# Five of eight layer-norm transposes moved from TensorE to the DMA queue

## The reference

```
h = layernorm(x)
Q, K, V = h Wq^T, ctx Wk^T, ctx Wv^T
x = x + tanh(g_xattn) * (softmax(causal(Q K^T / sqrt(128))) V) Wd^T
x = x + tanh(g_ffn) * (layernorm(x) W^T + bias)      W: 512x512, unpacked from 6-bit fields
```

## Time and profile before

| | |
|---|---|
| median of three runs | 1070.28 us (1069.42 to 1071.28) |
| the profiled execution's own time | 1069.89 us |
| its span in the profile | 1067.7 us, so 2.19 us lie around it |
| busy: PE, DVE, ACT, POOL | 1026.9, 677.1, 476.4, 235.3 us |

### The profile page before, as it was taken

The page is one execution under the profiler, slowest core; times in us unless marked ns, Lnnn a source line. Parts: engine busy times, 40 slices in busy tenths (PEclk is TensorE's granted clock), DMA queues, the critical chain, the costliest instruction groups (busy, mean ns, idle before and its releaser), DMA issues.

```text
span 1067.7 us, 20167 instructions
## 1 busy us (share of the span) xinstructions
PE 1026.9 (96%) x8002; PEld 577.5 (54%) x8002; DVE 677.1 (63%) x1364; ACT 476.4 (45%) x937; POOL 235.3 (22%) x245
## 2 busy tenths in 40 slices
PE   5889999999999999999999999999999999999995
PEld 2455555555555555555555555555555555555552
DVE  5856677776668556655566566555556664555578
ACT  5777676676434243343334323254433423333322
POOL 1355566566503100010003110010000400000003
PEclk9999999999999999999999999999999999999999
DMA  7747645445245133233321443312323332233211
GB/s 273 234 154 266 216 169 169 159 158 167 91 139 197 51 129 118 107 112 118 119 86 54 178 159 118 119 42 98 119 99 119 119 117 67 75 119 117 81 41 59
DMA packets 64250, 137.08 MB, mean 128 GB/s; under 512 B 5408, under 2 KB 38176, under 8 KB 53536
## 3 DMA queue, kind: packets, MB, share of 16 engines
q1 hardware_dynamic: 64160, 135.81, 37.2%
HBM read 93.85 MB, written 25.17 MB: 111 GB/s over the span
## 4 chain that ended last, share of the span: by engine, by line
PE 87%; DVE 7%; ACT 3%; issue 2%; DMA 1%; SPq 0%; POOL 0%; DVEq 0%; ACTq 0%; POOLq 0%
PE pa L1225 42%; PE py L1225 29%; PE av L1338 5%; PE pp L1321 3%; PE ps L1305 2%; PE py L1399 2%; PE pp L1305 2%; PE av L1375 1%; DVE q L843 1%; DMA raw_q<-in_wqT 1%; DVE sc L900 1%; DVE row_max L887 1%; DVE sc L889 1%; DVE sc L883 1%; DVE xh L1006 1%
## 5 line engine op out<-in xcount | busy, mean ns | idle before, releaser
L1225 PE MATMUL pa<-xT,wq 128*128 128x512 f16 x1536 | 342.7, 379 | 7.3 <-DVE q L843 4.5
L1225 PE MATMUL py<-wd,att 128*128 128x512 f16 x1488 | 337.0, 379 | 0.8 <-issue 0.8
L1225 PEld LDWEIGHTS pa<-xT,wq 128*128 128x128 f16 x1536 | 145.8, 98 | 187.6 <-issue 20.4
L1225 PEld LDWEIGHTS py<-wd,att 128*128 128x128 f16 x1488 | 142.9, 98 | 158.1 <-issue 1.1
L629 ACT ACTIVATE q<-pa 128x512 f16<-128x512 f32 x128 | 75.7, 592 | 246.6 <-PE pa L1225 246.6
L922 DVE SCALAR_TENSOR_TENSOR xacc<-py,f_y,xacc 128x512 f32<-128x512 f32 x128 | 95.8, 749 | 134.0 <-PE py L1225 134.0
L675 ACT ACTIVATE att<-av 128x256 f16<-128x256 f32 x256 | 80.8, 384 | 145.7 <-PE av L1338 145.3
L913 DVE SCALAR_TENSOR_TENSOR att<-av,att 128x256 f16<-128x256 f32 x256 | 93.5, 418 | 67.1 <-ACT att L675 66.9
L843 DVE SCALAR_TENSOR_TENSOR q<-pa,q 128x512 f16<-128x512 f32 x128 | 87.8, 686 | 63.6 <-ACT q L629 60.8
L1225 PE MATMUL pa<-wv,cT 128*128 128x128 f16 x1536 | 96.2, 219 | 0.0
L1225 PEld LDWEIGHTS pa<-wv,cT 128*128 128x128 f16 x1536 | 89.8, 98 | 0.9
(11 more groups left out here) (127 smaller groups left out, 1100.2 us busy)
## 6 DMA issues: line engine op xcount, KB each, us to landing
wq<-kept_q SPq DMA_DIRECT2D x24, 1024.0 KB, 7.2
wd<-kept_d SPq DMA_DIRECT2D x23, 1024.0 KB, 4.8
v_dup<-v_nat SPq DMA_DIRECT2D x128, 128.0 KB, 2.4
raw_d<-in_wdT SPq DMA_DIRECT2D x8, 1024.0 KB, 10.5
kept_q<-wq SPq DMA_DIRECT2D x8, 1024.0 KB, 7.5
kept_d<-wd SPq DMA_DIRECT2D x8, 1024.0 KB, 5.4
raw_q<-in_wqT SPq DMA_DIRECT2D x7, 1024.0 KB, 5.2
wk<-kept_k SPq DMA_DIRECT2D x24, 256.0 KB, 7.4
```

What stands on the lines that cost most here:

```text
L1225: last = pe.matmul(out, stationary(a, i), moving(b, i), start=(i == 0 and (a, b) == PASSES[0]), stop=(i == count - 1 and (a, b) == PASSES[ ...
```

## The change

Calls 2 to 6 of the norms are no longer transposed by PE (`BY_PE` keeps calls 0, 1 and 7). SP issues DMA transposes instead, from `xh` straight into `xT`: 8 a tile, two tiles in each of the two steps after the norm's own step, 16 in a step and 32 for a call, queued behind the reloads of that step's weights and ahead of `duplicate_v`. PE's 160 transposes of these calls and ACT's 20 copies out of `av` go. Whoever reads `xT` waits for the DMA semaphore `xT_ld` instead of `xT_ok`, and so does ACT before it overwrites `xh` in the next call. The FFNs of blocks 0 and 1 move from step 1 to step 3 of the pass, and their stores with them. The interleaving of the norms of kind 2 moves from the read of the transpose to the writes of `ln_hi` and `ln_lo` (views of innermost length 4, whose elements lie 128 apart).

```diff
+        FINAL = len(NORMS) - 1
+        BY_PE = (0, 1, FINAL)
...
+        def transposed(eng, call):
+
+            if call in BY_PE:
+                eng.wait_ge(xT_ok, tile_count(TILES * (call + 1) - 1) + 1)
+            else:
+                eng.wait_ge(xT_ld, 16 * 2 * KC * TILES * (call - 1))
...
+        def dma_tiles(n):
+
+            g, tb = n % GROUPS, n // GROUPS
+            if tb > 0 and g in (1, 2):
+                return NORMS.index((2, tb - 1)), (2 * g - 2, 2 * g - 1)
+            if 0 < tb < BLOCKS - 1 and g in (5, 6):
+                return NORMS.index((1, tb + 1)), (2 * g - 10, 2 * g - 9)
+            return None
...
-            if g == 1 and 0 < tb < BLOCKS - 1:
+            if g == 3 and 0 < tb < BLOCKS - 1:
                 return tb - 1
...
+            def transpose_tiles(call, tiles):
+
+                which, tb = NORMS[call]
+                if which == 1:
+                    sp.wait_ge(q_mm, 4 * GROUPS * (tb - 1))
+                    sp.wait_ge(f_mm, TILES * (tb - 1))
+                else:
+                    sp.wait_ge(q_mm, 4 * GROUPS * (tb + 1))
+                for t in tiles:
+                    sp.wait_ge(x_hi, TILES * call + t + 1)
+                    wait_x_lo(sp, TILES * call + t)
+                    for c in (HI, LO):
+                        for i in range(KC):
+                            sp.dma_start(xT[:, tb % 2, c, i, t * P:(t + 1) * P], xh[:, t, c, i * P:(i + 1) * P],
+                                         transpose=True).then_inc(xT_ld, 16)
...
                 if GROUPS <= m + 1 < STEPS:
                     back_qkv(m + 1)
+                if dma_tiles(n) is not None:
+                    transpose_tiles(*dma_tiles(n))
                 if m < STEPS:
                     duplicate_v(m)
...
+                return part.rearrange("p (j i) -> p i j", j=KC)
...
-                pool.tensor_tensor(xh[:, t % TILES, LO, :], xn[:, t % TILES, :], xh[:, t % TILES, HI, :],
-                                   ALU.subtract).then_inc(x_lo, 1)
+                pool.tensor_tensor(permuted(xh[:, t % TILES, LO, :], t), straight(xn[:, t % TILES, :], t),
+                                   permuted(xh[:, t % TILES, HI, :], t), ALU.subtract).then_inc(x_lo, 1)
...
+                if call in BY_PE:
                     for t in range(TILES):
                         ln_out(TILES * call + t)
...
-                        pe.wait_ge(xT_ok, TILES * (NORMS.index((1, tb)) + 1))
+                        transposed(pe, NORMS.index((1, tb)))
...
-                if call is not None:
+                if call in BY_PE:
                     ln_transpose(TILES * call, 4 * n + 4)
                     ln_transpose(TILES * call + 1, 4 * n + 4)
                 y_unit(n, 3)
-                if call is not None:
+                if call in BY_PE:
                     ln_transpose(TILES * call + 2, 4 * n + 4)
                     ln_transpose(TILES * call + 3, 4 * n + 4)
```

More of the change, by code:

```diff
@@ L176, in build @@
         xT_mm, xT_ok = sem("xT_mm"), sem("xT_ok")
+        xT_ld = sem("xT_ld")
         q_mm, q_hi, q_lo = sem("q_mm"), sem("q_hi"), sem("q_lo")
@@ L470, in split_wv, with permuted, straight @@
                 weight_lo(wv[:, g % 2, LO, :, :], raw_v[:, g % 2, :, :], wv[:, g % 2, HI, :, :], w_mul[:, g, 2:3], wv_lo)
+            def permuted(part, t):
+                if NORMS[t // TILES][0] == 1:
+                    return part
+                return part.rearrange("p (j i) -> p i j", j=KC)
+            def straight(part, t):
+                if NORMS[t // TILES][0] == 1:
+                    return part
+                return part.rearrange("p (i j) -> p i j", j=KC)
             def ln_lo(t):
                 pool.wait_ge(x_hi, t + 1)
-                pool.tensor_tensor(xh[:, t % TILES, LO, :], xn[:, t % TILES, :], xh[:, t % TILES, HI, :],
-                                   ALU.subtract).then_inc(x_lo, 1)
+                pool.tensor_tensor(permuted(xh[:, t % TILES, LO, :], t), straight(xn[:, t % TILES, :], t),
+                                   permuted(xh[:, t % TILES, HI, :], t), ALU.subtract).then_inc(x_lo, 1)
             def ln_rstd(call):
@@ L642, in v_part, with permuted, straight @@
                                scale=K_SCALE).then_inc(v_hi, 1)
+            def permuted(part, t):
+                if NORMS[t // TILES][0] == 1:
+                    return part
+                return part.rearrange("p (j i) -> p i j", j=KC)
+            def straight(part, t):
+                if NORMS[t // TILES][0] == 1:
+                    return part
+                return part.rearrange("p (i j) -> p i j", j=KC)
             def ln_hi(t, summed):
+                call = t // TILES
                 act.wait_ge(xn_ok, t + 1)
-                wait(act, xT_mm, t - TILES + 1)
-                at = NORMS[t // TILES][1] * TILES + t % TILES
-                act.activation(xh[:, t % TILES, HI, :], xn[:, t % TILES, :], ACT.Copy,
+                if call > 0 and t % TILES == 0:
+                    if call - 1 in BY_PE:
+                        act.wait_ge(xT_mm, tile_count(t - 1) + 1)
+                    else:
+                        transposed(act, call - 1)
+                at = NORMS[call][1] * TILES + t % TILES
+                act.activation(permuted(xh[:, t % TILES, HI, :], t), straight(xn[:, t % TILES, :], t), ACT.Copy,
                                accum_out=x_sum[:, at:at + 1] if summed else None).then_inc(x_hi, 1)
             def ln_out(t):
-                act.wait_ge(xT_mm, t + 1)
+                act.wait_ge(xT_mm, tile_count(t) + 1)
                 par = NORMS[t // TILES][1] % 2
@@ L1005, in ln_lo @@
                 dve.wait_ge(xn_ok, t + 1)
-                dve.tensor_tensor(xh[:, t % TILES, LO, :], xn[:, t % TILES, :], xh[:, t % TILES, HI, :],
-                                  ALU.subtract).then_inc(xd_lo, 1)
+                dve.tensor_tensor(permuted(xh[:, t % TILES, LO, :], t), straight(xn[:, t % TILES, :], t),
+                                  permuted(xh[:, t % TILES, HI, :], t), ALU.subtract).then_inc(xd_lo, 1)
             def ffn_weight(j):
@@ L1332, in av_unit @@
                 wait(pe, av_lo, 4 * n + j - 1)
-                if j < 2 and n > 0 and norm_of(n - 1) is not None:
-                    pe.wait_ge(xT_ok, TILES * (norm_of(n - 1) + 1))
+                if j < 2 and n > 0 and norm_of(n - 1) in BY_PE:
+                    transposed(pe, norm_of(n - 1))
                 for bb in range(2):
@@ L1363, in ln_transpose @@
                 wait_x_lo(pe, t)
-                wait(pe, xT_ok, t - 1)
+                wait(pe, xT_ok, tile_count(t) - 1)
                 wait(pe, av_hi, av_before)
@@ L1369, in ln_transpose @@
                     for i in range(KC):
[L1370 to L1373, removed]
+                        part = xh[:, t % TILES, c, i * P:(i + 1) * P]
                         at = (c * KC + i) * P
@@ L1380, in ffn_unit @@
                     pe.wait_ge(ffw_ok, 4)
-                if t % TILES == 0 and t not in FFN_DVE:
-                    pe.wait_ge(xT_ok, TILES * (NORMS.index((2, t // TILES)) + 1))
                 if t in FFN_DVE:
-                    pe.wait_ge(xT_ok, TILES * NORMS.index((2, t // TILES)) + t % TILES + 1)
+                    pe.wait_ge(xT_ok, tile_count(TILES * FINAL + t % TILES) + 1)
+                elif t % TILES == 0:
+                    transposed(pe, NORMS.index((2, t // TILES)))
                 if t == LATE[0]:
```

2 lines of the change are left out of this document (added).

## The result

The changed kernel takes 1079.79 us (median of four runs, 1078.74 to 1081.84), against 1070.3 for the kernel before: a ratio of 1.0091, interval 1.0072 to 1.0109. It is 0.9% slower, where 1057.4 us, so 1.2% faster, was forecast. The profiled execution took 1081.84 us.

What follows compares the result with a forecast made beforehand. PE was taken to bound the kernel: 1069.89 - 13.66 + 0 + 0.3 + 0.5 = 1057.0, median put at 1057.4 us. The likeliest case ran from 1054.5 to 1060, the wider range up to 1080.

Steps and rivals of the forecast that it cites:

- What leaves PE: Term: PE's transposes and waits at the ends of steps 8, 12, 16, 20 and 24 go, saving 13.66 us.
- What SP's queue takes on: Term: the DMA transposes on SP's queue lie hidden behind PE's products, at a cost of 0.
- T: Time one DMA transpose adds to SP's queue, taken as 0.65 to 1.3 us; 1.60 fills a step's room.
- a slow queue: Rival: PE waits at queries and FFNs if T is well over 1.64; chance 0.04 near break-even, 0.21 beyond.
- full DMA engines: Rival: T is engine time, engines full from T = 1.34, 1062 us at 1.41; chance 0.12 shared with DVE.
- The FFN's move: Term: FFN work joins a step with more DVE work, costing 0.3 us for two steps together.
- The interleaved writes: Term: writes of ln_hi and ln_lo, hidden in calls 2, 4 and 6, cost 0.5 us in call 7.
- The sign that the prediction named for this: Sign of being wrong: DVE's `ln_lo` in call 7 at over 1.3 us without POOL beside it.
- The upper bound, half speed: Call 7: single-element writes at half speed would add 2.7 us over DVE's four `ln_lo`.
- the rival that the prediction had for that end: Rival for ending slower: SP's queue too slow, 1156 us at T = 2.4; chance of slower 0.21.
- The gap stays: Rival: PE waits for DVE at y_unit 3 or step 3, 1064 us; chance 0.12 shared with full DMA engines.

Runs made afterwards that it cites:

- host order with later weights: host order, with DVE making the FFN's weights and rows one step later (end of step 9 instead of step 8); 1057.94 us, ratio 0.9858.
- host order: Changed kernel with inputs and output permuted on the host, so ACT, POOL and DVE read and write xh contiguously; 1059.58 us, ratio 0.9892.

## Why the prediction was wrong, point by point

- **What leaves PE**: right. 13.66 us were worked out from the ends of five steps, 13.58 measured, and y_unit 3 was not late after y_unit 2.
- **What SP's queue takes on**: right. T was 1.27 to 1.37, at and just above the upper end of the 0.65 to 1.3 taken and under the 1.60 to 1.64 at which the first wait was due; steps 13 to 15 and 21 to 23 are 30.27 us each. The run with 32 in one step shows that the limit exists. The rivals of a slow queue (0.25 of the chance) and of full DMA engines did not come; the second was hardly tested, since a call's mean T was 1.32 and its first wait was due at 1.34.
- **The FFN's move**: right, 0.3 us taken for both. In host order with later weights steps 9 to 11 and 17 to 19 take 98.42 and 97.87 us, for 97.86 and 97.85 before; the 0.56 is step 10, where the unpacking now lies.
- **The interleaved writes**: this step failed, in two of its sentences. "I lean to the low end: 0.5 us" for call 7 rested on PE's strided read, which says nothing of a write by another engine; the tail lost 8.14 us, 6.7 of them against host order. The sign that the prediction named for this came: `ln_lo` in call 7 took 4.82 / 2 = 2.41 us, most of that without POOL beside it, so that its four together took 9.64 us for 5.22 before. And "The interleaved writes of ACT and POOL in calls 2, 4 and 6 have a step's end to hide behind" priced them at nothing: steps 9, 17 and 25 lost 5.97 + 3.60 + 3.60 = 13.2 us to them against host order. The upper bound, half speed, was itself an assumption without a row; the real price was a quarter of the speed on ACT, and DVE's operations stood still beside POOL's. So the run ended slower, but not by the rival that the prediction had for that end; no chance stood for this one.
- **The gap stays**: this rival came at one place. Before, PE's transposes in step 8 (2.92 us) and the FFN's matmuls between the queries of step 9 lay over DVE's unpacking of weights; both have gone from there, and step 9 is 1.93 us longer than a plain step in host order. Moving the unpacking took it away. No run takes the one cover away without the other. The rival looked for DVE at y_unit 3 or in step 3, not at the queries behind the unpacking.

With the writes contiguous and the unpacking a step later the kernel runs at 1057.94 us, beside the 1057.4 predicted; so the rest of the sum held. That the two agree to 0.5 us is in part luck: the move of the unpacking takes out a wait that the prediction did not know of. What stays open: why the clock falls after some waits of 2 us and not after others, what part of a write's price is distance and what the length of its runs, and on POOL and DVE what part is the write and what the interleaved read of the high part.

## What to carry to other kernels

A permutation has to be paid somewhere: moving it from PE's read, where it cost at most 0.3 us a call (2.92 and 2.73 us in steps 8 and 16 beside 2.64 in step 12), to the writes of other engines made three engines' work two to four times as long. Give such an edit a price from both sides on every engine that it touches, and look at what else runs then on the neighbours (here VectorE's casts beside GpSimd), not only at whether the operation itself has time. Where the layout of inputs is free, permute there; where it isn't, the four-byte read was the next best place here (1063.43 beside 1059.58 us).

## What the runs showed of the hardware

- Two-byte writes 256 bytes apart took 2.3 us of ACT's time a tile (0.63 contiguous), 2.4 on DVE (0.68) and 2.3 to 2.6 on POOL (1.15); on DVE and POOL the operation also read two-byte elements at that distance.
- A shift and a cast on DVE went from 0.42 and 0.43 us to 2.0 to 2.2 and 2.58 beside POOL's interleaved writes (the cast to 1.26 beside contiguous ones); the product of a scalar and two tensors that adds `py` to `xacc` kept its 0.73 beside them.
- A DMA transpose of 128x128 two-byte elements took 1.23 us of SP's queue (median of 160) and 2.3 us to land, so the next one is issued before the last has landed. All 160 add 25,600 packets under 512 bytes (5408 to 31008).
